# Four transformer blocks on one Trainium2 core: the reads of q and k in pieces of 16 rows and the rest

## The chip, the cores and the metric

The kernel runs on one core of one Trainium2 chip. The metric is the device time of one execution in microseconds; times here are the median of three runs. A core has TensorE (matrix products), VectorE, ScalarE and GpSimd for the rest of the arithmetic, SyncE (SP), which in this kernel does nothing but issue transfers and wait, and sixteen DMA engines that move the bytes.

## The reference

The input is 32 sequences of 128 tokens with 144 channels, and one condition vector for each sequence. Four blocks follow one another. Each one computes six modulation vectors from the condition, then attention with 16 heads of 9 dimensions, then an MLP with 576 hidden channels:

```python
q, k, v = qkv[0], qkv[1], qkv[2]          # from modulate(norm(x)) @ w_qkv + b_qkv
attn = softmax(einsum('bhqd,bhkd->bhqk', q, k) * hd ** -0.5)
o = einsum('bhqk,bhkd->bhqd', attn, v) ...
x = x + g_msa * (o @ w_proj + b_proj)
x = x + g_mlp * mlp(modulate(norm(x)))
```

Layer 0 has a mixture of four experts, two for each token, in place of the MLP. Layer 2 normalises with the root of the mean square, also q and k of each head. In layer 3 attention goes over the 16 heads of one token, `einsum('nthd,ntkd->nthk', q, k)`, so the kernel computes it for 8 tokens at once with a mask, and rearranges q, k and v through memory in pieces of 32 values.

## The kernel before, in words

The 32 sequences stay in the on-chip memory (`X`) through all four layers. They are worked in groups of four sequences, 8 groups a layer, so 32 groups over the kernel, numbered n = 0 to 31. The order of the work is written out by hand for each engine.

For attention, TensorE makes q and k with 96 rows of (dimension, head) by 512 tokens. Each value is cut into three bfloat16 parts (`parts`), whose products together give the accuracy of float32. The scores of one head then need the parts of q and k of that head on neighbouring partitions: a combination of six pairs of parts times 9 dimensions, 54 rows. That rearrangement goes through memory. `write_parts(l, n)` (line 398) writes `parts` to `qk_scr` (to `tok_scr` in layer 3), SP waits until the writes have landed (line 433), and `read_parts(l, n)` (line 421) reads them back into `qk`, for each half s (heads 0 to 7 on partitions 0 to 53, heads 8 to 15 on partitions 64 to 117) and each side (q, k). `RUNS` says which parts follow one another on the 54 rows: for q it is a run of 2 parts, one of 3 and one of 1, for k of 3, 1 and 2, with 9 rows a part. A run is one transfer, of 18, 27 or 9 rows. In the first three layers a row is 8 KB in one piece; in layer 3 it is eight pieces of 1 KB. One group has 3 x 2 x 2 = 12 read transfers and 216 rows.

`qk` has three places (n % 3), and a read is issued two groups ahead of its use. TensorE waits for both halves before the first scores of a group (`scores_for_max`, the matmuls of line 648), and `write_parts` two groups later waits for them before it overwrites the memory. Both waits are for the count that `fetched(n)` gives: each transfer adds 16 to the semaphore of its place and half.

SP's queue in a group of attention is: write the parts, wait for them, read them, in layer 3 wait for the v of the group and read it back turned (`turn_values`, line 451), load the gates (line 394), and in some groups weights (lines 344 to 356). In layer 3 ScalarE issues the writes of v (`v_scr`), and SP's wait for them is line 450.

Of the kernel before, what the change touches and what calls it, by code (L numbers as in the profile page):

```python
# [16 lines left out]
H, D = 16, 9  # L17
# [89 lines left out]
def build(nc, io):  # L107
    ctx = ExitStack()
    with ctx:
# [3 lines left out]
        def sem(name):  # L113
            return ctx.enter_context(nc.semaphore(name))
# [130 lines left out]
        q_r = [[sem(f"q_r{r}{s}") for s in range(2)] for r in range(3)]  # L245
# [38 lines left out]
        def written(n):  # L284
            return 64 * (n + 1) if n < 24 else 64 * 24 + 192 * (n + 1 - 24)

        def fetched(n):
            return 96 * (n // 3 + 1)

        def normal(k):  # L290

# [16 lines left out]
        def _(sp):  # L308
# [89 lines left out]
            def write_parts(l, n):  # L398
                p = n % 2
                if n >= 2:  # L400
                    for s in range(2):
                        sp.wait_ge(q_r[(n - 2) % 3][s], fetched(n - 2))
                for m in range(3):
                    sp.wait_ge(a_p1, CR + 3 * n + m + 1)
                    sp.wait_ge(g_p2, CR + 3 * n + m + 1)
                    sp.wait_ge(g_p3, CR + 3 * n + m + 1)
                    for side in range(2):
                        a = max(0, QK_DIMS * m - D * side)
                        b = min(D, QK_DIMS * (m + 1) - D * side)
                        if a >= b:  # L410
                            continue
                        r0 = H * (a + D * side) - QK_ROWS * m
                        src = parts[r0:r0 + H * (b - a), m]
                        if l < 3:
                            sp.dma_start(qk_scr[p, side, :, a:b].rearrange("a d h t -> (d h) a t"), src).then_inc(q_w, 16)
                            continue
                        for part in range(3):
                            sp.dma_start(tok_scr[p, side, :, :, part, a:b].rearrange("c b d h w -> (d h) (c b) w"),  # L418
                                         src[:, part].rearrange("r (a w) -> r a w", w=32)).then_inc(q_w, 16)

            def read_parts(l, n):
                p, r = n % 2, n % 3
                if 1 <= n < 3:
                    sp.wait_ge(d_mod, CR + L)
                    sp.wait_ge(s_mod, CR + L)
                if n >= 3:
                    sp.wait_ge(s_st, CR + 8 * (n - 2))
                    sp.wait_ge(s_sm, CR + 8 * (n - 2))
                if n == 26:
                    sp.wait_ge(s_v, CR + 2 * 26)  # L430
                if n in (8, 10):
                    sp.wait_ge(d_hg, CR + NT * (1 if n == 8 else 8))
                sp.wait_ge(q_w, written(n))
                for s in range(2):
                    for side, runs in enumerate(RUNS):
                        row = 64 * s
                        for first, many in runs:
                            if l < 3:
                                src = qk_scr[p, side, first:first + many, :, 8 * s:8 * s + 8].rearrange("a d h t -> (a d) (h t)")
                                dst = qk[row:row + many * D, side, r].rearrange("r h t -> r (h t)")  # L440
                            else:
                                src = tok_scr[p, side, 2 * s:2 * s + 2, :, first:first + many] \
                                    .rearrange("c b a d h w -> (a d) (c b) (h w)")
                                dst = qk[row:row + many * D, side, r]
                            sp.dma_start(dst, src).then_inc(q_r[r][s], 16)  # L445
                            row += many * D

            def turn_values(n):
# [17 lines left out]
            def attention(l):  # L466
                n0, m0 = 8 * l, 16 * l
                if l == 0:
                    write_parts(0, 0)
                    read_parts(0, 0)  # L470
                    for i in range(L):
                        save_gates(i)
                    write_parts(0, 1)
                    read_parts(0, 1)
                    sp.wait_ge(q_gs[0], 16)
                    load_gates(0)
                    sp.dma_start(X[:, 4 * G:B, :], xv[:, 4 * G:B, :]).then_inc(q_x4, 16)
                    for i in range(NEAR, NST + NEAR):
                        load_chunk(i)
                    for i in range(1, L):  # L480
                        sp.wait_ge(q_gs[i], 16)
                if l == 2:
                    write_parts(l, n0 + 1)
                    read_parts(l, n0 + 1)
# [57 lines left out]
        def _(pe):  # L542
# [97 lines left out]
            def scores_for_max(l, U):  # L640
                n = U // UNITS
                pe.wait_ge(d_sm, CR + U)
                if U % UNITS == 0:
                    for s in range(2):
                        pe.wait_ge(q_r[n % 3][s], fetched(n))
                for i in range(4):
                    for s in range(2):
                        mm = pe.matmul(bank[s][:, T * i:T * i + T], operand(l, 0, n, U, s, i),  # L648
                                       operand(l, 1, n, U, s, i), start=True, stop=True)
                mm.then_inc(s_sm, 1)  # L650
# [1462 lines left out]
```

## Time and profile before

| | |
|---|---|
| median of 3 runs | 1574.65 us (1568.06 to 1575.15) |
| profiled execution | 1567.82 us, span 1566.0 us |
| mean granted TensorE clock | 0.956 of full speed |
| busy share: VectorE, ScalarE, GpSimd | 66%, 50%, 35% |
| moved by DMA | 134.92 MB, 86 GB/s over the span |
| packets under 512 B | 142461 of 209128 |

The profile is one execution. Its span runs from the first to the last instruction, and every row below gives times from the start of the span. The DMA share is the mean busy share of the sixteen DMA engines; it can be a little over 1 because the packets of one engine overlap.

### The profile page before, as it was taken

The page shows a single profiled execution, that of the slowest core. Times are in us where ns is not written, and L with a number is a line of the kernel's source. Part 1 is how long each engine was busy: PE and PEld are TensorE (multiplying, and loading weights), DVE is VectorE, ACT ScalarE, POOL GpSimd, SP SyncE. Part 2 cuts the span into 40 slices and gives each one's busy share as a digit, 9 for nine tenths or more (in the row PEclk, how much of TensorE's full clock was granted, in tenths as well). Part 3 has the DMA queues.
Part 4 walks back from the last instruction along what each step waited for, and adds up shares of the span by engine and source line. Part 5 has one row for each costly group of instructions (what it writes and reads, how often), then busy time and mean ns, then how long its engine had stood idle before and what let it go on. Part 6 is the DMA issues. An engine that isn't in the chain of part 4 may idle for free. (4 is left out here: it accounts for less than half of the span.)

```text
span 1566.0 us, 41002 instructions
## 1 busy us (share of the span) xinstructions
PE 1427.5 (91%) x15976; PEld 1076.4 (69%) x15976; DVE 1038.6 (66%) x2592; ACT 781.2 (50%) x1287; POOL 543.8 (35%) x739
## 2 busy tenths in 40 slices
PE   6799988999999998998999778877999799998998
PEld 2477776777777776766776557666777577767776
DVE  4688874766676677878547679887446466665342
ACT  2377753333323336766645356665544265655443
POOL 3355532211131213544324323443335244342322
PEclk9799999999999999999999888998999799999999
DMA  4665631111022123554001333443116667774021
GB/s 131 159 152 145 160 79 52 50 43 43 35 68 71 38 67 81 147 131 131 17 31 35 107 88 93 108 118 98 33 36 88 110 102 111 137 134 93 17 61 46
DMA packets 209128, 134.92 MB, mean 86 GB/s; under 512 B 142461, under 2 KB 191320, under 8 KB 202730
## 3 DMA queue, kind: packets, MB, share of 16 engines
q1 hardware_dynamic: 188978, 129.74, 34.8%
q10 hardware_dynamic: 19960, 2.57, 1.2%
q8 instruction: 129, 2.11, 0.6%
q14 instruction: 61, 0.50, 0.1%
HBM read 98.24 MB, written 33.24 MB: 84 GB/s over the span
## 5 line engine op out<-in xcount | busy, mean ns | idle before, releaser
L1530 DVE TENSOR_REDUCE negm<-banks 128x8 bf16<-128x1024 f32 x256 | 311.2, 1216 | 88.7 <-PE banks L648 86.4
L1221 ACT ACTIVATE prob<-banks 128x1024 f32<-128x1024 f32 x256 | 262.3, 1025 | 212.7 <-PE banks L670 211.8
L1348 ACT ACTIVATE hid<-banks 128x512 f32<-128x512 f32 x144 | 85.9, 597 | 230.4 <-PE banks L949 230.4
L1947 POOL TENSOR_TENSOR X<-X,gx 128x288 f32<-128x288 f32 x128 | 104.9, 832 | 266.5 <-DVE gx L1560 264.7
L666 PE MATMUL banks<-qk 54*128 54x128 bf16 (+1 forms) x2048 | 172.3, 239 | 6.8 <-ACT prob L1221 5.0
L965 PEld LDWEIGHTS banks<-wfc,hid 128*128 128x128 f32 x1152 | 157.1, 190 | 30.0 <-issue 19.9
L670 PE MATMUL banks<-mT,identb 64*128 64x128 bf16 x2048 | 168.8, 228 | 0.0
L965 PE MATMUL banks<-wfc,hid 128*128 128x144 f32 x1152 | 161.5, 286 | 0.0
L648 PE MATMUL banks<-qk 54*128 54x128 bf16 (+1 forms) x2048 | 124.9, 245 | 39.7 <-DVE negm L1530 21.9
L948 PE MATMUL banks<-hT,wfc 128*128 128x512 f32 x288 | 149.0, 599 | 1.8 <-DMA wfc<-in_L_cond_w 1.3
L682 PE MATMUL banks<-prob,V 128*32 128x128 f32 x4096 | 148.4, 289 | 0.0
L1718 DVE TENSOR_TENSOR hid<-hid,qk 128x512 f32<-128x512 f32 x128 | 88.9, 695 | 88.8 <-ACT hid L1348 80.3
L1468 DVE TENSOR_SCALAR hmod<-banks,modr 64x128 f32<-64x128 f32 x256 | 86.8, 395 | 76.8 <-PE banks L581 76.4
L1932 POOL CAST parts<-res 96x512 bf16<-96x512 f32 x96 | 58.6, 611 | 212.3 <-DVE res L1481 211.4
L1373 ACT ACTIVATE hid<-banks 128x512 f32<-128x512 f32 (+1 forms) x120 | 71.1, 596 | 122.0 <-PE banks L939 121.6
L985 PE MATMUL banks<-wfc,hid 128*128 128x144 f32 (+1 forms) x960 | 130.5, 293 | 0.2 <-DVE gx L1560 0.2
L985 PEld LDWEIGHTS banks<-wfc,hid 128*128 128x128 f32 (+1 forms) x960 | 126.1, 196 | 3.8 <-issue 2.7
L648 PEld LDWEIGHTS banks<-qk 54*128 54x128 bf16 (+1 forms) x2048 | 71.1, 103 | 83.3 <-issue 38.6
L938 PE MATMUL banks<-hT,wfc 128*128 128x512 f32 x240 | 123.5, 595 | 0.0
L682 PEld LDWEIGHTS banks<-prob,V 128*32 128x32 f32 x4096 | 110.5, 115 | 17.9 <-issue 7.4
L666 PEld LDWEIGHTS banks<-qk 54*128 54x128 bf16 (+1 forms) x2048 | 110.4, 103 | 10.7 <-ACT prob L1221 7.3
L1934 POOL TENSOR_TENSOR parts<-res,parts 96x512 bf16<-96x512 f32 x96 | 112.9, 1176 | 7.9
(165 smaller groups left out, 2789.9 us busy)
## 6 DMA issues: line engine op xcount, KB each, us to landing
qk<-qk_scr SPq DMA_DIRECT2D x96, 216.0 KB
gbuf<-gate_scr SPq DMA_DIRECT2D x64, 288.0 KB, 4.2
qk_scr<-parts SPq DMA_DIRECT2D x48, 288.0 KB, 2.9
qk<-qk_scr SPq DMA_DIRECT2D x96, 144.0 KB
qk<-cw_scr SPq DMA_DIRECT2D x8, 1024.0 KB, 4.6
qk_scr<-parts SPq DMA_DIRECT2D x48, 144.0 KB, 2.4
qk<-qk_scr SPq DMA_DIRECT2D x96, 72.0 KB
qk<-tok_scr SPq DMA_DIRECT2D x32, 216.0 KB
```

The costliest lines, as they stand in the source:

```text
L648: mm = pe.matmul(bank[s][:, T * i:T * i + T], operand(l, 0, n, U, s, i), operand(l, 1, n, U, s, i), start=True, stop=True)
L666: pe.matmul(bank[2 + s][:, at], operand(l, 1, n, U, s, i), operand(l, 0, n, U, s, i), start=True, stop=False)
L670: mm = pe.matmul(bank[2 + s][:, at], one_hot(half, 64 * s + 4 * (u % 2) + i, [64, T]), mT[half, u // 2, :], start=False, stop=True)
L682: mm = pe.matmul(bank[4][32 * i:32 * i + 32, T * (2 * s + u % 2):T * (2 * s + u % 2 + 1)], V[:, n % 3, u // 2, VS * h:VS * h + 32], prob[: ...
L938: pe.matmul(bank[2 + i % 2][:], wfc1_t[:, at:at + 128], hT[:, h, :], start=True, stop=False)
L948: pe.matmul(bank[2 + i % 2][:], w, hT[:, h, :], start=True, stop=False)
L965: mm = pe.matmul(bank[4 + b // 2][:, C * (b % 2):C * (b % 2) + C], hid[:, i % KT, T * b:T * b + T], wfc2[:, e - (t == KT - 1), t, :], star ...
L985: mm = pe.matmul(bank[4 + q][:, C * (b % 2):C * (b % 2) + C], hid[0:rows, t, T * b:T * b + T], wfc2[0:rows, k, t, :], start=(t == 0), stop ...
L1221: act.activation(prob[:, 2 * (U % 3):2 * (U % 3) + 2, :], pairs[1][:], ACT.Exp, scale=scale).then_inc(a_exp, 1)
L1530: dve.tensor_reduce(negm[:, u // 2, :, 4 * (u % 2):4 * (u % 2) + 4], pairs[0][:].rearrange("q s (h k) -> q s h k", k=T), AX.X, ALU.max, ne ...
L1934: pool.tensor_tensor(parts[:, m, 2, :], res[:, i % 2, :], parts[:, m, 1, :], ALU.subtract).then_inc(g_p3, 1)
L1947: pool.tensor_tensor(x, x, gx[:, q, :, :], ALU.add).then_inc(g_x, 1)
```

## The change

A run of more than one part is no longer read by one transfer. It is cut after its 16th row: 27 rows become 16 and 11, and 18 become 16 and 2. A run of 9 rows stays whole. A group then has 5 transfers instead of 3 for each half and side, 20 instead of 12, and the count waited for rises accordingly. The rows, their places and their bytes are the same.

```diff
         def fetched(n):
-            return 96 * (n // 3 + 1)
+            return 160 * (n // 3 + 1)
...
                                 dst = qk[row:row + many * D, side, r]
-                            sp.dma_start(dst, src).then_inc(q_r[r][s], 16)
+                            for rows in (slice(0, 16), slice(16, many * D)) if many > 1 else (slice(0, D),):
+                                sp.dma_start(dst[rows], src[rows]).then_inc(q_r[r][s], 16)
                             row += many * D
```

On SP, the read of the first group begins as follows before the change. `18x4096` is a transfer of 18 rows of 4096 values; the rows shown are half 0 and the first of half 1.

```order
L445 DMA qk<-qk_scr 18x4096
L445 DMA qk<-qk_scr 27x4096
L445 DMA qk<-qk_scr 9x4096
L445 DMA qk<-qk_scr 27x4096
L445 DMA qk<-qk_scr 9x4096
L445 DMA qk<-qk_scr 18x4096 x2
```

The same place in the changed kernel, half 0 alone:

```order
L446 DMA qk<-qk_scr 16x4096
L446 DMA qk<-qk_scr 2x4096
L446 DMA qk<-qk_scr 16x4096
L446 DMA qk<-qk_scr 11x4096
L446 DMA qk<-qk_scr 9x4096
L446 DMA qk<-qk_scr 16x4096
L446 DMA qk<-qk_scr 11x4096
L446 DMA qk<-qk_scr 9x4096
L446 DMA qk<-qk_scr 16x4096
L446 DMA qk<-qk_scr 2x4096
```

Six transfers of a half have become ten, and the order of the runs is the same.

The second place is SP's queue behind a read of layer 3, group 29, before the change. `hid<-v_scr` is the read of the turned v, `gbuf` holds the gates, and `wfc` is a weight.

```order
L445 DMA qk<-tok_scr 27x8x512
L445 DMA qk<-tok_scr 9x8x512
L445 DMA qk<-tok_scr 18x8x512
L451 DMA hid<-v_scr 36x4x512
L394 DMA gbuf<-gate_scr 128x576
L349 DMA wfc<-in_L_cond_fc_w 128x4x144
```

And in the changed kernel:

```order
L446 DMA qk<-tok_scr 16x8x512
L446 DMA qk<-tok_scr 11x8x512
L446 DMA qk<-tok_scr 9x8x512
L446 DMA qk<-tok_scr 16x8x512
L446 DMA qk<-tok_scr 2x8x512
L452 DMA hid<-v_scr 36x4x512
L394 DMA gbuf<-gate_scr 128x576
L349 DMA wfc<-in_L_cond_fc_w 128x4x144
```

What is queued behind the read stays in its order and stands eight transfers later. The other engines' instructions are the same in kind and order.

## Rows read from the trace of the kernel before

**Rows 1.** The page: busy us of each engine, share of the span, instructions.

```profile
PE 1427.5 (91%) x15976; PEld 1076.4 (69%) x15976; DVE 1038.6 (66%) x2592; ACT 781.2 (50%) x1287; POOL 543.8 (35%) x739
```

**Rows 2.** Waits of PE: line, waited for: us in total, times, longest us.

```profile
PE banks L655 <- DVE On L1548: 42.7, 39, 4.3
PE banks L648 <- DVE negm L1530: 21.9, 23, 4.8
PE banks L648 <- DMA qk<-qk_scr: 8.6, 4, 3.2
PE banks L648 <- DMA qk<-tok_scr: 7.1, 3, 3.5
```

**Rows 3.** Timeline of PE: start us, us, instruction, [idle before <- releaser].

```profile
99.24 0.40 PE L648 MATMUL banks<-qk 54*128 54x128 bf16 x8 [1.48 <-DMA qk<-qk_scr]
213.50 0.49 PE L648 MATMUL banks<-qk 54*128 54x128 bf16 x8 [2.50 <-DMA qk<-qk_scr]
743.83 0.40 PE L648 MATMUL banks<-qk 54*128 54x128 bf16 x8 [1.41 <-DMA qk<-qk_scr]
1092.39 0.61 PE L648 MATMUL banks<-qk 54*128 54x128 bf16 x8 [3.19 <-DMA qk<-qk_scr]
1374.82 0.64 PE L648 MATMUL banks<-qk 62*128 62x128 bf16 x8 [2.32 <-DMA qk<-tok_scr]
1404.31 0.64 PE L648 MATMUL banks<-qk 62*128 62x128 bf16 x8 [1.27 <-DMA qk<-tok_scr]
1434.09 0.65 PE L648 MATMUL banks<-qk 62*128 62x128 bf16 x8 [3.48 <-DMA qk<-tok_scr]
```

**Rows 4.** Windows: stretch, engines' busy us, then PEclk, DMA share, GB/s.

```profile
741.20:743.80 2.60, 0.23 (x1) 0.10 (x1) 1.68 (x5) 0.38 (x1) 0.00 (x0) 1.00 0.13 34
212.00:213.50 1.50, 0.00 (x1) 0.03 (x1) 0.00 (x0) 0.00 (x0) 0.00 (x0) 1.00 0.37 107
865.00:877.50 12.50, 11.23 (x60) 8.04 (x59) 9.12 (x29) 5.62 (x14) 1.85 (x4) 1.00 0.55 142
250.00:251.00 1.00, 1.00 (x3) 0.48 (x3) 0.00 (x0) 0.43 (x1) 0.00 (x0) 1.00 0.96 401
10.00:12.00 2.00, 2.00 (x4) 0.33 (x4) 0.00 (x0) 0.00 (x0) 0.00 (x0) 1.00 1.07 353
198.00:203.00 5.00, 4.90 (x107) 4.42 (x109) 4.90 (x14) 3.44 (x6) 4.03 (x6) 1.00 0.57 159
203.00:208.00 5.00, 4.60 (x97) 3.46 (x93) 4.50 (x10) 3.35 (x5) 1.71 (x3) 1.00 0.89 173
110.00:114.00 4.00, 3.67 (x89) 2.99 (x84) 3.40 (x6) 2.88 (x4) 3.23 (x6) 1.00 0.95 172
```

**Rows 5.** Timeline of SP's queue: issues of a read, and what follows one.

```profile
864.17 4.33 SPq L445 DMA_DIRECT2D qk<-qk_scr  x12
1360.11 5.61 SPq L445 DMA_DIRECT2D qk<-tok_scr  x12
1370.38 0.29 SPq L451 DMA_DIRECT2D hid<-v_scr  x1
```

**Rows 6.** Line 445: issues, ns min/median/max of one, first and last start.

```profile
L445 SPq DMA_DIRECT2D qk<-qk_scr x288: 270/316/1250, 35.1 to 1082.0; - x144
```

**Rows 7.** Waits of SP's queue.

```profile
SPq L394 <- DVE gx L1560: 358.8, 27, 30.2
SPq L406 <- POOL parts L1934: 147.4, 64, 19.0
SPq L450 <- DMA v_scr<-wfc: 43.7, 6, 9.5
```

**Rows 8.** Chain that ended last, around group 31: start us, us, what.

```profile
1392.88 9.72 DMA v_scr<-wfc
...
1418.61 0.27 SPq L445
...
1424.45 9.50 DMA qk<-tok_scr
```

## The prediction

> **What bounds the kernel now.** I first read the busy times of the page: TensorE is busy 91% of the span and the next engine 66% [rows 1], so what the span can lose quickly is idle time of TensorE. I then asked what TensorE waits for [rows 2]. The longest waits are for VectorE (42.7 us on `On`, 21.9 us on `negm`), and the change touches neither. Waits for the reads of q and k come to 8.6 us in the first three layers (4 times) and 7.1 us in the last (3 times), 15.7 us or 1.0% of the span. The seven waits one by one are in [rows 3]; the reader is to look at the number in brackets, the idle time in front of the first scores of a group. They are 1.48, 2.50, 1.41, 3.19, 2.32, 1.27 and 3.48 us. The other 25 of the 32 groups have their q and k in time. So whatever happens to the reads, a gain is bounded by about 15.7 us, while a loss is bounded by nothing so small, since all 32 groups could come to wait.
>
> One of the seven doesn't count. In front of 743.83 the DMA engines are already nearly empty from 741.20 on (share 0.13) [rows 4], 2.6 us before TensorE starts. That read had landed, and the wait is put down to it only because no later releaser is on record. The others are real: in front of 213.50, for one, 212.00 to 213.50 still has a share of 0.37 and 107 GB/s [rows 4]. That leaves six, with 14.2 us.
>
> Next I asked how long a read takes. The cleanest one is issued from 864.17 on [rows 5], and from 865.00 to 877.50 it is nearly alone: 12.5 us at 142 GB/s, which is its 216 rows of 8 KB (1.77 MB) [rows 4]. I take 12.6 us. The waited reads are no shorter: the last one lasts from its first issue at 1418.61 to its landing at 1433.95, 15.3 us [rows 8].
>
> **The share of the DMA engines tells how many of them work.** In the clean read it is 0.55 [rows 4]; 0.55 x 16 is 8.8, so nine engines carry the read. Nine is also the largest number up to sixteen that divides 27, 18 and 9. Where tensors of 128 rows move, the share is 0.96 (the gates spread over all rows, 401 GB/s) or 1.07 (the first weights, 353 GB/s) [rows 4]: all sixteen. Read so, a transfer of 16 rows takes sixteen engines, one of 11 rows eleven, one of 2 rows two.
>
> The Trainium skill states this rule, in "DMA: Bandwidth & Descriptors", section "Why a DMA increments its semaphore by 16 and not by 1": the number of engines is the largest up to 16 that divides the slowest dimension of both sides. By that rule the trace agrees, with nine busy engines.
>
> **The change part by part.** (a) Load per engine. For each half and side there are now 2 + 3 + 1 = 6 rows on each of nine engines, 24 a group. Afterwards the first two engines carry 1 + 1 + 1 + 1 + 1 = 5 rows for each half and side, 20 a group, the next seven 16, and the last five 8. If the rate of one engine is the limit, a read shrinks by 4/24 of 12.6 us, 2.1 us.
>
> Is that rate the limit? 142 GB/s over 8.8 engines is 16 GB/s for each. In the spreading of the gates it is 401 / (0.96 x 16) = 26 GB/s for each [rows 4]. So an engine in these reads runs at 0.62 of what it can do: it is held up by something the nine have in common. A stretch where the other seven have work too says the same: from 203 to 208, while gates and weights move beside the read, the share rises to 0.89 but the rate only from 159 to 173 GB/s, and from 110 to 114 it is 0.95 with 172 GB/s [rows 4]. Half as many engines again gave 9% more bytes. What all these reads have in common is that they write 54 neighbouring partitions of one half of the memory at a time; the weights, with 353 GB/s, write 128.
>
> The Trainium skill has a rule for this that speaks against the change, in "SBUF — State Buffer", section "Door 1: The DMA port swizzle": the DMA side has 16 ports, four neighbouring partitions and the four that lie 32 further share one, and partitions 0 to 63 reach only eight. By its figures (about 436 GB/s over 16 ports, 27 GB/s for one) the busiest port takes 8 rows for each half and side, 32 rows of 8 KB a group, in about 9.6 us as an estimate, however many engines send. The sum would be 0 to -3 us a read by it, against -2.1 by load; no run here has shown it yet.
>
> So what a read's length becomes is not shown by the trace before. The bound below is -2.1 us (load alone). The bound above is one where a transfer costs the same whatever its size: 12.6 / 12 = 1.05 us each, eight more of them, +8.4 us. I take -0.5 us, near the stretches of 159 to 173 GB/s, which let a fuller set of engines have a little more.
>
> (b) Issue. SP issues 12 transfers in 4.33 us [rows 5], 0.36 us each (median 316 ns and a gap) [rows 6]. Eight more are 2.9 us; in the last layer, at 5.61 us for 12 [rows 5], up to 3.7 us. The issue of 20 ends at 20 x 0.36 = 7.2 us, in the last layer at 9.4 us; the first packets move 0.9 us after the first issue (864.17 to 865, rows 4 and 5), and the read itself needs 12 us, so the issue lies beside the packets and doesn't set the landing. Cost: 0.
>
> (c) What is queued behind it on SP: the load of the gates, weights, in the last layer the read of the turned v (L451), then the next writes. All of these start 2.9 to 3.7 us later where SP was not waiting. But it mostly waits: 358.8 us for `gx` and 147.4 us for `parts` in one of its waits [rows 7]. The gates queue behind the read's packets on the engines anyway. In the last layer SP is the chain: v to memory (9.72 us), then the writes of q and k and their landing, the read (9.50 us after its last issue) [rows 8]. There it waits for v in front of L451, 43.7 us over 6 groups [rows 7], 7.3 us on average; the issue of one read ends at 1365.72 and L451 starts at 1370.38 [rows 5], 4.66 us later. 3.7 us fits under that. Cost: 0; if that cover were gone, up to 3.7 us for each of the three waited groups of this layer, 11 us.
>
> (d) No instruction of TensorE, VectorE, ScalarE or GpSimd changes, and the counts waited for are raised with the number of transfers (5 x 2 sides x 16 = 160 for 3 x 2 x 16 = 96), so no wait is added.
>
> **The sum.** Six waited reads x -0.5 us = -3.0 us, and 0 for the rest. The profiled execution took 1567.82 us (span 1566.0 us), which makes 1564.8 us. The median of the three runs before is 1574.65 us, 6.8 us above the profiled one, and I put the forecast on that scale: 1574.65 - 3.0, rounded, 1571.6 us.
>
> **The rivals.** *The engines' load is the limit after all.* Each read takes 2.1 us less, and each wait shrinks by the smaller of itself and 2.1: 1.48 + 2.1 + 2.1 + 2.1 + 1.27 + 2.1 = 11.2 us. Something is late next in part of them (VectorE's `negm` is waited for 23 times, rows 2), so about 10 us: 1564.6 us. For it: the share of 0.55 shows seven idle engines. Against it: 16 GB/s for an engine that does 26 elsewhere.
>
> *The rows collide.* A transfer of 16 rows sends sixteen engines at 16 neighbouring rows at once, where nine engines now start three rows apart over 27. If what is shared is a path into neighbouring partitions, as the low rate suggests, the crowding costs more than the four rows save, and eight more transfers add starts and completions. A read that takes 2.0 us more (a quarter of the way to +8.4) makes all seven waits of rows 3 longer by 2.0 us, 14 us: 1588.6 us. It decides from the point where a read takes longer than 12.6 us plus what little is left before TensorE asks, which is nothing at six places. For it: 0.89 of the engines busy gave 173 GB/s, 12 GB/s each. Against it: bytes in total did not fall there. By the section on the ports named above, such a transfer would use four ports, which is the worst case of that rule.
>
> *The change doesn't spread.* Engines stay as many as now, for instance because the division follows something else than the rows; then only (b) and (c) remain, and the time is that of before, 1574.65 us.
>
> **How the numbers follow.** Forecast (reads 0 to 1 us shorter) 0.5, load as the limit 0.2, collision 0.2, no spreading 0.1. A difference under 0.5%, 7.9 us, can't be told from none here. Faster by more: 0.7 of the load case and a tenth of the forecast's, 0.19. Slower by more: 0.8 of the collision case, 0.16. Within: 0.65. The forecast alone has 1566 to 1578 us, given that the three runs before lie 7.1 us apart. The range of 8 in 10 takes in the load case down to 1560 us and the collision case up to 1585 us.
>
> **What would show it.** The share of the DMA engines in a clean read (the one near 865 us) should rise from 0.55, first near 1 and then falling, while its rate stays between 140 and 175 GB/s: then the shared limit is right. If the read ends within 10.5 us at 170 GB/s or more, the load case is right; over 14 us, the collision. SP should show 20 issues in about 7 us. The waits for `qk` should stay near 15.7 us with the forecast, fall to about 5 with the first rival and rise towards 30 with the second. In the last layer L451 should still be released by v: if SP comes to it late instead, (c) was wrong. The forecast as a whole is wrong if the reads' length stays and the time still moves by over 8 us.

## The result, and the profile after

| | before | after |
|---|---|---|
| median of 4 runs, same chip | 1571.36 us (1567.2 to 1575.15) | 1618.28 us (1614.0 to 1621.12) |
| profiled execution | 1567.82 us, span 1566.0 us | 1617.82 us, span 1616.0 us |
| mean granted TensorE clock | 0.956 | 0.944 |

The ratio is 1.0309 [1.0279, 1.034]: the change makes the kernel 3.1% slower. The forecast was 1571.6 us with a range of 1560 to 1585 us; it was wrong, and the time lies far above even the collision rival's 1588.6 us.

The busy times of the page after, to compare with [rows 1]:

```profile
PE 1443.0 (89%) x15976; PEld 1085.7 (67%) x15976; DVE 1039.2 (64%) x2592; ACT 780.4 (48%) x1287; POOL 542.5 (34%) x739
```

What TensorE waits for (line, waited for: us in total, times, longest us), to compare with [rows 2]; the scores are now line 649:

```profile
PE banks L656 <- DVE On L1549: 43.6, 40, 4.3
PE banks L649 <- DMA qk<-qk_scr: 31.8, 14, 5.9
PE banks L649 <- DVE negm L1531: 22.1, 24, 4.6
PE banks L649 <- DMA qk<-tok_scr: 15.6, 4, 7.0
```

The waits for VectorE have hardly moved. The waits for reads of q and k have gone from 15.7 us in 7 places to 47.4 us in 18. That is 31.7 of the 50.0 us by which the profiled executions differ. TensorE's busy time rose by another 15.5 us (1427.5 to 1443.0) with the same 15976 instructions, at a mean clock of 0.944 in place of 0.956: 1427.5 x 0.956 / 0.944 is 1445.6, so the lower clock is large enough to account for it. Together that is 47.2 of 50.0 us. The clock granted behind a long new wait is low. At the first scores of group 2, which wait 1.48 us before and 5.03 us after, it is 1.00 before and 0.50 after:

```profile
99.20:101.20 2.00, 1.96 (x57) 1.69 (x58) 1.23 (x1) 1.03 (x2) 1.55 (x2) 1.00 0.56 172
103.50:105.50 2.00, 1.93 (x36) 1.73 (x40) 1.22 (x1) 0.43 (x1) 0.00 (x0) 0.50 0.64 220
```

So a new wait can cost more than its own length. Not all of the 15.5 us need be of that kind: by the tables of stages below 11.6 us of them lie in the four stretches that hold the reads. The mean clock also differs between executions of one kernel, from 0.944 to 0.949 for the change and, in a kernel with no longer waits than before (e5 below), from 0.946 to 0.957.

The first scores of some groups on TensorE's timeline (start us, us, instruction, [idle before <- releaser]), to compare with [rows 3]:

```profile
103.57 0.61 PE L649 MATMUL banks<-qk 54*128 54x128 bf16 x8 [5.03 <-DMA qk<-qk_scr]
223.46 0.61 PE L649 MATMUL banks<-qk 54*128 54x128 bf16 x8 [3.42 <-DMA qk<-qk_scr]
644.84 0.40 PE L649 MATMUL banks<-qk 54*128 54x128 bf16 x8 [2.34 <-DMA qk<-qk_scr]
1129.17 0.61 PE L649 MATMUL banks<-qk 54*128 54x128 bf16 x8 [5.94 <-DMA qk<-qk_scr]
1484.04 0.64 PE L649 MATMUL banks<-qk 62*128 62x128 bf16 x8 [6.99 <-DMA qk<-tok_scr]
```

Four of the five are in the place of one of before: 1.48 us became 5.03, 2.50 became 3.42, 3.19 became 5.94, 3.48 became 6.99. The one at 644.84 is new, as are ten others. There the same eight matmuls take 0.40 us behind a wait of 2.34 us, and 0.61 us at 103.57 behind one of 5.03 us, where they took 0.40 before [rows 3].

Where in the program the time went, by stage. The columns are those of [rows 4]. A packet is counted in the stretch in which it starts, with all its time and bytes, so share and rate of a stretch of one or two microseconds are rough. Each stretch runs from the first scores of a layer's first group to those of its last. Before, layers 0 to 3:

```profile
53.60:213.50 159.90, 141.57 (x2495) 106.25 (x2495) 133.64 (x273) 104.00 (x151) 78.40 (x99) 0.95 0.62 152
...
893.60:1092.40 198.80, 154.99 (x2578) 125.19 (x2579) 168.88 (x392) 117.24 (x195) 71.43 (x112) 0.88 0.40 104
```

And after:

```profile
54.10:223.50 169.40, 142.88 (x2496) 107.32 (x2498) 133.78 (x273) 103.99 (x151) 78.88 (x100) 0.94 0.78 144
591.30:764.80 173.50, 153.82 (x2563) 116.20 (x2562) 134.51 (x268) 106.14 (x155) 74.83 (x96) 0.97 0.58 111
916.40:1129.20 212.80, 159.30 (x2578) 128.20 (x2580) 169.07 (x392) 116.98 (x195) 71.24 (x112) 0.85 0.52 98
1265.70:1484.00 218.30, 193.76 (x2585) 144.09 (x2584) 131.06 (x266) 110.93 (x163) 75.38 (x99) 0.91 0.78 114
```

Attention of layer 0 took 159.90 us and takes 169.40, that of layer 2 took 198.80 and takes 212.80; layers 1 and 3 (166.30 and 204.90 us before) take 7.2 and 13.4 us more. That is 44 of the 50 us in the four stretches that hold the reads. The DMA share rose in each, from 0.62 to 0.78 in layer 0, while the rate fell from 152 to 144 GB/s: the engines are busy longer with fewer bytes a second.

The read of group 16, before in [rows 4] from 865.00 on:

```profile
889.70:905.90 16.20, 14.92 (x92) 11.84 (x92) 11.71 (x41) 7.03 (x16) 3.05 (x9) 1.00 0.78 128
```

It takes 16.2 us in place of 12.5, with a share of 0.78 in place of 0.55. But its row is no longer of the read alone. SP issues the load of the gates 11.7 us after the read's first issue, and 113 of its 128 packets start before the read ends; in the kernel before its packets came when the read was over. The read's own 1.77 MB in 16.2 us are 109 GB/s, not 128. The next read, of group 17, has nothing beside it in either kernel. Before, as a whole, its first ten microseconds and the rest:

```profile
895.80:908.10 12.30, 4.99 (x70) 3.24 (x72) 8.85 (x14) 1.02 (x1) 0.00 (x0) 0.52 0.54 140
895.80:905.80 10.00, 3.20 (x42) 1.98 (x44) 7.13 (x12) 0.00 (x0) 0.00 (x0) 0.53 0.57 147
905.80:908.10 2.30, 1.79 (x33) 1.26 (x30) 1.72 (x3) 1.02 (x1) 0.00 (x0) 0.50 0.43 107
```

And after:

```profile
919.20:935.20 16.00, 9.34 (x119) 6.76 (x123) 12.55 (x23) 3.32 (x5) 0.00 (x0) 0.50 0.71 110
919.20:929.20 10.00, 3.84 (x50) 2.36 (x50) 7.20 (x11) 0.00 (x0) 0.00 (x0) 0.50 0.89 139
929.20:935.20 6.00, 5.50 (x69) 4.40 (x73) 5.35 (x14) 3.32 (x5) 0.00 (x0) 0.50 0.41 63
```

It takes 16.0 us in place of 12.3, so the gates aren't the reason. The rows to look at are the two of ten microseconds. With 0.89 of the sixteen engines busy they move 139 GB/s, where nine engines (0.57) moved 147: many more engines at work, and no more bytes. What is left after ten microseconds then goes slowly, 63 GB/s at a share of 0.41.

From the packet records, each read from its first to its last packet (216 rows, or 1728 pieces of 1 KB in layer 3): a read of the first three layers lasts 13.46 us on average before and 16.25 us after, one of layer 3 13.2 and 15.6 us. The mean packet of 8 KB stays on its engine for 526 ns before and 799 ns after. These two numbers nearly give the length of a read: the busiest engine had 24 rows and now has 20 by the prediction's count, and as an estimate 24 x 526 ns is 12.6 us and 20 x 799 ns is 16.0 us. The load fell by a sixth, and each packet takes half as long again.

SP's queue, to compare with [rows 5], and its line in the form of [rows 6]:

```profile
888.78 7.27 SPq L446 DMA_DIRECT2D qk<-qk_scr  x20
1402.59 8.39 SPq L446 DMA_DIRECT2D qk<-tok_scr  x20
1412.24 0.29 SPq L452 DMA_DIRECT2D hid<-v_scr  x1
L446 SPq DMA_DIRECT2D qk<-qk_scr x480: 220/308/1685, 35.6 to 1119.1; - x160
```

SP's waits, to compare with [rows 7]:

```profile
SPq L394 <- DVE gx L1561: 362.1, 27, 30.3
SPq L451 <- DMA v_scr<-wfc: 31.3, 6, 8.5
```

And the chain that ended last at group 31, to compare with [rows 8], where the last step was 9.50 us:

```profile
1473.29 10.61 DMA qk<-tok_scr
```

### The profile page after: what moved, and what is told of

Same layout as the page of the kernel before. It is cut to its first block and busy times, and to the rows that moved or that the text cites. A ratio compares the mean times of both kernels' runs of the same rounds, so it can differ in the third digit from the quotient of the medians.

```text
span 1616.0 us, 41258 instructions
## 1 busy us (share of the span) xinstructions
PE 1443.0 (89%) x15976; PEld 1085.7 (67%) x15976; DVE 1039.2 (64%) x2592; ACT 780.4 (48%) x1287; POOL 542.5 (34%) x739
## 5 line engine op out<-in xcount | busy, mean ns | idle before, releaser
L649 PE MATMUL banks<-qk 54*128 54x128 bf16 (+1 forms) x2048 | 126.2, 247 | 71.5 <-DMA qk<-qk_scr 31.8
L667 PE MATMUL banks<-qk 54*128 54x128 bf16 (+1 forms) x2048 | 174.9, 240 | 7.8 <-ACT prob L1222 5.0
L683 PE MATMUL banks<-prob,V 128*32 128x128 f32 x4096 | 153.8, 295 | 0.4 <-issue 0.4
L683 PEld LDWEIGHTS banks<-prob,V 128*32 128x32 f32 x4096 | 113.9, 117 | 19.7 <-issue 8.9
L667 PEld LDWEIGHTS banks<-qk 54*128 54x128 bf16 (+1 forms) x2048 | 112.5, 104 | 11.2 <-ACT prob L1222 7.3
L1165 ACT ACTIVATE hT<-banks,modm 128x128 f32<-128x128 f32 x256 | 99.5, 453 | 34.9 <-PE banks L575 34.9
```

Source lines behind the costliest of these rows:

```text
L667: pe.matmul(bank[2 + s][:, at], operand(l, 1, n, U, s, i), operand(l, 0, n, U, s, i), start=True, stop=False)
L683: mm = pe.matmul(bank[4][32 * i:32 * i + 32, T * (2 * s + u % 2):T * (2 * s + u % 2 + 1)], V[:, n % 3, u // 2, VS * h:VS * h + 32], prob[: ...
L1165: act.activation(hT[:, slot_of(k), T * b:T * b + T], bank[o][:, T * b:T * b + T], ACT.Identity, scale=modm[:, l, 2 * w + 1, at:at + 1], bi ...
```

## The experiments

Each was timed against the kernel before on its own chip, and each diff is against the kernel before. Read lengths and packet times are means worked out from the packet records as above; the waits are TensorE's in front of the scores (in e5 and e8 the trace puts them down to the tiny transfers, which count on the same semaphore). A table first, to have the sizes side by side:

| kernel | ratio to before | read, layers 0 to 2 | 8 KB packet | waits |
|---|---|---|---|---|
| before | 1 | 13.5 us | 526 ns | 15.7 us |
| the change | 1.0309 [1.0279, 1.034] | 16.25 | 799 | 47.4 |
| e1_nine_pieces | 1.025 [1.0206, 1.0295] | 16.0 | 629 | 31.7 |
| e2_spread_sixteen | 1.0492 [1.0446, 1.0537] | 16.2 | 443 | 64.9 |
| e3_spread_nine | 1.0016 [0.9995, 1.0037] | 13.4 | 432 | 15.4 |
| e4_one_source_row | one run, 1638.52 us | 16.7 | 830 | 54.8 |
| e5_eight_tiny | 1.0033 [1.0003, 1.0062] | 13.7 | 526 | 15.6 |
| e8_slow_issue | one run, 1638.12 us | 17.4 | 734 | 64.3 |
| e6_halves_in_turn | 0.991 [0.9887, 0.9933] | 11.9 | 468 | 4.2 |
| e7_sixteen_in_turn | 1.0081 [1.0055, 1.0107] | 15.4 | 754 | 26.0 |
| e9_crossed | 0.994 [0.9918, 0.9962] | 12.3 | 481 | 3.0 |
| e10_only_27 | 1.0077 [1.0046, 1.0108] | 14.25 | 652 | 18.4 |
| e11_only_18 | 1.0277 [1.024, 1.0314] | 15.9 | 672 | 38.3 |
| e12_ten_eight | 1.0086 [1.0059, 1.0113] | 14.4 | 565 | 22.9 |
| e13_even_cuts | 1.0278 [1.0237, 1.0319] | 16.2 | 728 | 38.9 |
| e14_turn_15_12 | 0.9963 [0.9936, 0.999] | 13.3 | 618 | 7.9 |

**Twenty transfers, nine engines.** Is it the sixteen engines? The runs are cut at their last 9 rows, so every transfer has 9 or 18 rows.

```diff
+for rows in (slice(0, many * D - D), slice(many * D - D, many * D)) if many > 1 else (slice(0, D),):
+    sp.dma_start(dst[rows], src[rows]).then_inc(q_r[r][s], 16)
```

> Twenty transfers a group as in the changed kernel, but cut after a multiple of nine rows (27 = 18 + 9, 18 = 9 + 9), so that nine engines carry each one. Theory N (each further transfer costs by itself, in issue and completion): as slow as the changed kernel, about 1.03 of before, a clean read of about 16 us. Theory D (sixteen engines at sixteen neighbouring partitions at once crowd the way into them): about the time of before, ratio 1.00 to 1.01, a clean read of 12.5 to 13.5 us at a DMA share of 0.55.

Measured: 1603.86 us, and a read of group 16 of 17.0 us:

```profile
885.80:902.80 17.00, 15.73 (x96) 12.54 (x95) 12.25 (x42) 7.75 (x18) 3.11 (x5) 1.00 0.62 119
```

Theory D in this form, which ties the crowd to sixteen engines, is refuted, and theory N has its numbers; it falls with e5 below. Nine engines with equal loads are nearly as slow as sixteen with unequal ones. So neither the number of engines nor the uneven load is needed for the loss. In these pieces of 9 rows nine engines write nine neighbouring partitions at a time. That in a run of 27 rows they stand three apart is the prediction's reading; the packet records name neither engine nor partition.

**The destinations spread.** The 54 rows of a half are laid on every third partition, in pieces of up to 16 rows, or of up to 18 rows (nine engines). q and k are laid out alike, so the scores are the same sums.

```diff
+at = 0
+while at < many * D:
+    c, i = divmod(row - 64 * s, 18)
+    m = min(many * D - at, 18 - i)
+    m = 16 if m == 18 else m          # e2 only
+    p0 = 64 * s + c + 3 * i
+    dst = qk[p0:p0 + 3 * m - 2:3, side, r]
```

> Pieces of 16, 2 and 9 rows, twenty-four transfers a group, with the 54 rows laid in every third partition (row 18c + i of a half on partition c + 3i, for q and k alike, so the scores are the same), so that sixteen engines write to partitions three apart over 46. Theory D: the read falls well under the changed kernel's 16.1 us, to 10 to 13 us, and the ratio to before is at or below 1.01. Theory N: slower still than the changed kernel, 1.03 to 1.05, reads of 17 us or more. Theory S (the source: sixteen neighbouring rows of memory at once are slow): as the changed kernel, 1.03.

> Same spread partitions, nine engines, pieces of 18 and 9 rows, sixteen transfers a group. Theory D: the transfers of 9 rows no longer meet on three groups of four partitions, a clean read falls from 12.5 us to 11 to 12 us, ratio 0.992 to 1.000. Theory N: four more transfers than before, a quarter to a half of the changed kernel's loss, 1.01 to 1.015. If the neighbours of a partition play no part at all: 12.5 us and 1.00.

Measured: 1642.6 and 1570.05 us. The first doesn't test what it was made for, and SP's issues show why (the second line is the same of e2 as [rows 5]):

```profile
L451 SPq DMA_DIRECT2D qk<-qk_scr x576: 496/622/1527, 35.3 to 1133.3; - x192
899.05 15.64 SPq L451 DMA_DIRECT2D qk<-qk_scr  x24
```

A transfer that steps three partitions at its destination takes SP 622 ns to issue instead of 316, so 24 of them take 15.6 us, and the 16.2 us of the read are the issue. For e3 the issue of 16 takes 11.90 us, and its read of group 16 takes 12.9 us, not the 11 to 12 us of theory D. What both do show is the packet: with destinations three apart, 443 ns for 8 KB with sixteen rows to a transfer and 432 ns with nine engines, against 799 and 526. But packets that come slowly meet less company, which needs a control.

**The control: the change's pieces, issued slowly.** Behind each of the twenty transfers a tiny one (2 rows of 8 bytes) is issued.

```diff
+sp.dma_start(dst[rows], src[rows]).then_inc(q_r[r][s], 16)
+bit = src[0:2, 0:4] if l < 3 else src[0:2, 0, 0:4]
+sp.dma_start(tiny[:, c:c + 4], bit).then_inc(q_r[r][s], 16)
```

> The changed kernel with a tiny transfer (2 rows of 8 bytes) behind each of its twenty, so that the pieces of 16 rows on neighbouring partitions are issued at about 0.66 us each, the pace of the kernel with spread partitions and sixteen engines. There a packet of 8 KB took 443 ns on average, against 799 ns in the changed kernel. Theory D: packets stay at 650 to 800 ns here. If the slow issue alone had relieved them: 430 to 500 ns. The time is bound by 40 issues, 13 us and more a read, in either case, 1615 to 1660 us.

Measured, in one run: 1638.12 us, packets of 734 ns, though the issue of a read is stretched to 13.0 us. e2, at 15.9 us for 24 transfers, has nearly the same pace (0.66 us each against 0.65) and 443 ns. So the neighbourhood of the destinations lengthens the packets, and the pace is a small part. That the read itself got longer (17.4 us) speaks against a cure by slower issue.

**One source row for all.** The change's pieces, but each transfer reads its first row again and again. The values of q and k are therefore not the reference's.

```diff
+one = src[rows.start:rows.start + 1].to_broadcast([rows.stop - rows.start] + list(src.shape[1:]))
+sp.dma_start(dst[rows], one).then_inc(q_r[r][s], 16)
```

> The changed kernel with every read transfer taking all its rows from its first source row: same transfers, same destination partitions, only one row of memory a transfer is read, so the values of q and k are not the reference's. Theory S: the reads fall to 8 to 11 us and the time to 1565 us or less. Theories D and N: the reads stay at about 16 us and the time at 1600 to 1620 us.

Measured, in one run: 1638.52 us, packets of 830 ns, read 16.7 us. The time lies 20 us above the change, beyond what any theory had. It is no better than the change, so where the rows lie in memory isn't the cause, if a single repeated row is not itself a difficulty. It isn't: when the gates are spread (one 8 KB row to 128 partitions by sixteen engines, the 401 GB/s of [rows 4]), a packet takes 309 ns in the median and 344 ns on average. A single source row with neighbouring destinations takes 830 ns. That leaves the destination.

**Eight more transfers, tiny.** The twelve reads as before, with eight transfers of 9 rows of 16 bytes among them.

```diff
+if many > 1:
+    bit = src[0:D, 0:8] if l < 3 else src[0:D, 0, 0:8]
+    sp.dma_start(tiny[:, j:j + 8], bit).then_inc(q_r[r][s], 16)
```

> The kernel before, with its twelve transfers untouched, and eight tiny ones beside them (9 rows of 16 bytes each, after every transfer of 18 or 27 rows, to a spare place), so twenty transfers a group are issued and counted as in the changed kernel. Theory N (a transfer costs by its issue, start and completion, whatever it carries): most of the changed kernel's loss, 1.02 to 1.03, reads of 15 to 16 us. Theory D (crowding: which partitions the engines write at the same time): no more than the spread of the runs, 1.00 to 1.005, reads of 13 to 14 us with packets of about 530 ns.

Measured: ratio 1.0033 [1.0003, 1.0062], packets 526 ns, clean read 12.4 us:

```profile
872.40:884.80 12.40, 11.13 (x59) 7.94 (x59) 9.12 (x29) 5.51 (x14) 2.25 (x5) 1.00 0.54 142
```

The row is that of before. The count of transfers, with its issue and its waits, is worth at most 0.6%; the 1.05 us for a transfer that made the upper bound is ruled out.

**The halves in turn.** If neighbouring destinations are what is crowded, transfers to the two halves of the partitions should go beside each other better than two to the same half. Only the order of the twelve transfers changes: half 0 and half 1 alternate.

```diff
-for s in range(2):
-    for side, runs in enumerate(RUNS):
+for side, runs in enumerate(RUNS):
+    for first, many in runs:
+        for s in range(2):
```

> The kernel before with the same twelve transfers in another order: a run of half 0 (partitions 0 to 53), then the same run of half 1 (64 to 117), instead of all of half 0 first. Theory D, if the crowding is on paths that the two halves don't share: reads fall from 13.4 to 10 to 12 us and the ratio is 0.985 to 0.998. Theory N, or a crowding that the halves share: 13.4 us and 1.00.

Measured: 1556.88 us, ratio 0.991 [0.9887, 0.9933]. It beats both kernels. Two reads of it, groups 16 and 17:

```profile
862.90:874.20 11.30, 10.03 (x52) 6.94 (x51) 8.74 (x29) 5.55 (x14) 1.67 (x4) 1.00 0.52 155
892.20:902.70 10.50, 4.31 (x58) 2.69 (x58) 7.29 (x11) 0.57 (x1) 0.00 (x0) 0.50 0.53 165
```

and what is left of the waits:

```profile
PE banks L649 <- DMA qk<-qk_scr: 2.4, 1, 2.4
PE banks L649 <- DMA qk<-tok_scr: 1.8, 1, 1.8
```

Still nine engines (0.52 x 16 is 8.3), the same bytes, and 155 to 165 GB/s. The waits fall by 11.5 us and the profiled time by 12.0 us (1567.82 to 1555.85); the medians are 14.0 us apart (1570.86 and 1556.88). It is more than the 10 us of the prediction's most favourable rival, and without a further engine. The Trainium skill's rule in "SBUF — State Buffer", "Door 1: The DMA port swizzle", agrees in direction: halves have ports of their own. The prediction's estimate by its figures, 9.6 us for one half after the other, doesn't give the change's loss, since the same rows go to the same ports before and after, and the reads take 13.5 and 16.25 us.

**The change with the halves in turn, and with the sides crossed.** e7 is the change's twenty pieces in the order of e6. e9 is the twelve whole transfers, alternating, with q going to one half while k goes to the other.

```diff
+# e7
+for rows in (slice(0, 16), slice(16, many * D)) if many > 1 else (slice(0, D),):
+    for s in range(2):
+# e9
+for turn in range(2):
+    for j in range(3):
+        for s in range(2):
+            side = (turn + s) % 2
```

> The changed kernel with its twenty transfers in another order: a piece of half 0, then the same piece of half 1. Theory D with separate paths of the halves: reads fall from 16.1 us to 12 to 14 us, ratio 1.00 to 1.015. Theory N: 16 us and 1.03.

> Twelve transfers, half 0 and half 1 in turn, and in addition the sides crossed: while half 0 reads a run of q, half 1 reads the run of k at the same place (18 beside 27, 27 beside 9, 9 beside 18), so that two transfers that follow one another differ in their rows too. If only the alternation of the halves counts: as that kernel, reads of about 11.9 us and 0.991. If the two transfers of 9 rows following one another were still a crowd (9 engines on 3 groups of four partitions): reads of 10.5 to 11.5 us and 0.986 to 0.991.

Measured: e7 1.0081, e9 0.994. The order alone takes back 2.3 of the change's 3.1%, but its packets remain at 754 ns and its reads at 15.4 us (13.3 us in layer 3), where theory D had 12 to 14 us. e9's interval [0.9918, 0.9962] overlaps e6's: crossing the sides adds nothing.

**Which cut?** Only the 27s are cut (16 and 11), or only the 18s (16 and 2), 16 transfers in either case.

```diff
+for rows in (slice(0, 16), slice(16, many * D)) if many == 3 else (slice(0, many * D),):   # e10
+for rows in (slice(0, 16), slice(16, many * D)) if many == 2 else (slice(0, many * D),):   # e11
```

> Only the runs of 27 rows are cut (16 and 11), those of 18 stay whole, sixteen transfers a group. Theory D (a piece with one neighbouring row for each engine is the crowd): the cut puts 27 of the 54 rows into such pieces, beside the 9 that already were, so about 27/43 of the changed kernel's lengthening, reads near 15 us, ratio 1.013 to 1.022.

> Only the runs of 18 rows are cut (16 and 2), those of 27 stay whole, sixteen transfers a group. Theory D: 18 of 54 rows move into such pieces, a smaller lengthening than with the 27, reads near 14.3 us, ratio 1.005 to 1.015. The two together should about make the changed kernel's 1.031.

Measured: 1.0077 and 1.0277, reads of group 16 of 14.7 and 16.0 us. Theory D had the larger loss at the 27s, and it is the other way round: the cut of the 18s alone makes nine tenths of the whole loss. Its waits are:

```profile
PE banks L649 <- DMA qk<-qk_scr: 24.1, 11, 6.0
PE banks L649 <- DMA qk<-tok_scr: 14.2, 3, 6.6
```

Only a part of e10's loss is waits for reads: they rise by 2.7 us, the profiled time by 11.2 us, and 5.8 us more is idle time of TensorE for which the profile names no releaser ("issue"). What that is stays open.

The packet records have a candidate for e11. If row j of a transfer goes to engine j (the records don't name the engine), pieces of 2 rows give their work to engines 0 and 1. In e11 these carry 24 rows a read, the next seven 20, and seven engines 4. In the last three microseconds of the read of group 16, 5.3, 2.5 and 1.2 engines are busy and 8, 5 and 4 rows are finished, where before has 9.1, 8.6 and 5.8 busy and finishes 18, 18 and 14.

**The same cuts without the pieces of 2.** e12 cuts 18 into 10 and 8 alone; e13 does that and cuts 27 into 15 and 12, twenty transfers again.

```diff
+for rows in (slice(0, 10), slice(10, 18)) if many == 2 else (slice(0, many * D),):   # e12
+cut = {1: D, 2: 10, 3: 15}[many]                                                     # e13
+for rows in (slice(0, cut), slice(cut, many * D)) if many > 1 else (slice(0, D),):
```

> Only the runs of 18 rows are cut, but into 10 and 8 instead of 16 and 2; 27 stay whole, sixteen transfers a group as with the cut into 16 and 2, which took 1.028 of before. Theory D (one neighbouring row for each engine is a crowd): 18 of 54 rows are in such pieces in both kernels, so about the same here, reads of 15 to 16 us, 1.02 to 1.03. Theory T (the pieces of 2 rows leave a tail: engines 0 and 1 carry 24 rows, the other seven 20, and at the end only two engines work): no tail here, since engines 0 to 7 carry 24 each, so reads near 13.5 us and 1.000 to 1.010.

> Both runs cut without small remainders: 27 = 15 + 12 and 18 = 10 + 8, twenty transfers, all with one neighbouring row for each engine; engines 0 to 7 carry 20 rows, engine 8 has 16. Theory D: as the changed kernel, reads near 16 us, 1.025 to 1.035. Theory T: reads near 14 us, 1.005 to 1.015, as when only the 27 are cut.

Measured: 1.0086 and 1.0278, with reads of group 16 of

```profile
868.90:882.80 13.90, 12.63 (x71) 9.44 (x71) 10.06 (x32) 6.99 (x17) 2.89 (x5) 1.00 0.55 132
```

and

```profile
889.80:906.50 16.70, 15.42 (x96) 12.29 (x95) 11.71 (x41) 7.03 (x16) 3.55 (x9) 1.00 0.70 124
```

With 10 and 8 in place of 16 and 2 the loss falls from 2.8 to 0.9% (e11 against e12), and the thin tail is gone from the records of e12. That is what theory T had, but it doesn't show the tail to be the cause: the cut also sends ten engines at once instead of sixteen, and the packets are shorter, 565 against 672 ns. The busiest engines have 24 rows in both, and 24 x 565 ns is 13.6 us, 24 x 672 ns 16.1 us as an estimate, near the reads of 14.4 and 15.9 us. And e13 is as slow as the change within 0.3%, without a piece of 2 rows: its last microseconds have 8.0, 8.0, 3.7 and 0.6 engines busy with 8, 8, 9 and 2 rows finished, so that a packet of its pieces of 8 rows takes a full microsecond. A tail of two rows isn't needed for a loss; whether it makes one by itself is not shown. The parts don't add up either: 0.8 and 0.9% make 2.8% (e10, e12, e13, though e13 cuts the 27s at another row than e10), 0.8 and 2.8% make 3.1% (e10, e11, the change).

**The best order with a mild cut.** The 27s cut into 15 and 12, halves in turn.

```diff
+for rows in (slice(0, 15), slice(15, 27)) if many == 3 else (slice(0, many * D),):
+    for s in range(2):
```

> Halves in turn (0.991 of before, reads of 11.9 us on nine engines) and the 27 rows cut into 15 and 12, so that nine engines carry 20 instead of 24 rows and the others help. If the load of nine engines has become the limit once the halves alternate: reads of 10 to 11 us, 0.985 to 0.991. If neighbouring single rows crowd here too: reads of 12.5 to 14 us, 0.995 to 1.01.

Measured: 0.9963 [0.9936, 0.999], packets 618 ns, reads of 13.3 us, as by crowding. Worse than e6 without any cut, whose interval lies wholly below. No cut that was tried beats the whole runs in the same order.

## Why the prediction was wrong

**What bounds the kernel, and what the waits allow.** Right, but for the count of places in the sum. TensorE and its waits set the time, and 31.7 of the 50.0 us are those waits. The sentence that a loss is bounded by nothing so small was the one to weigh: 11 groups that had not waited now do. Counting from the packet records, 6 groups of before had their last row within 1 us of TensorE's use, and 19 after. The slack could have been read before the change: about 1 us passes between the last packet and the first scores even in a group that waits, and 22 of the 32 groups had less than 3.7 us, so that a read longer by 2.8 us reaches them. The sum had six. That one of the seven waits was not real is borne out: the last packet of the read in front of 743.83 ended at 741.23. After the change this group's last row is within 1 us too, and it waits 2.63 us.

**(a) The read.** This is the step that failed. The prediction took -0.5 us a read; measured are +2.8 us (13.46 to 16.25), and 3.7 us in the reads of groups 16 and 17. Its first half was right: the engines are held up by something they have in common, since the share rose to 0.71 in the read of group 17 and the rate didn't rise with it, and e4 and e5 leave the destination for it. The second half was wrong: it took the common limit as a fixed rate that a fuller set of engines keeps or betters, from stretches in which seven other engines worked on gates and weights, that is, on other partitions. At 203 to 208 "half as many engines again gave 9% more bytes" [rows 4] doesn't speak of sixteen engines that all write neighbouring partitions. With those the rate of the first ten microseconds was 139 in place of 147 GB/s, and over the whole read 110 in place of 140, as the packets took 799 in place of 526 ns.

Two slips in its working change nothing. The list of loads leaves out two engines, which have 12 rows a group. And the 32 rows for "the busiest port" add up both halves, which by the Trainium skill's section cited there have different ports: a port takes 16 rows a group, and 9.6 us holds only for one half after the other.

**(b) Issue.** Right: 20 issues in 7.27 us (7.2 forecast), in the last layer 8.39 us (9.4 forecast), and e5, with twenty issues but the reads uncut, is 0.3% slower. It would not have been for a stepping destination (e2).

**(c) The queue behind on SP.** Right in its cost. In the read at 1402.59 the issue ends at 1410.98 and line 452 is issued at 1412.24, 1.3 us later. SP still waits for v 6 times, 31.3 us in all (43.7 before), so it comes late in no group where it was early. That is 12.4 us less, no more than the 16.7 us that six reads with 2.8 us more of issue each could take from it. That the gates queue behind the read's packets was not so in the read of group 16, where they ran beside its last four microseconds; the read of group 17 was as much longer without them.

**(d) No other change.** Right for the instructions (15976 on TensorE). Not named there: TensorE's mean clock fell from 0.956 to 0.944, and 15.5 us of busy time came with it, most of it in the stretches with the longer waits. The sum had no such term, and every rival's price lacked it as well.

**The rivals.** Load as the limit: refuted, the read got longer although the busiest engine has 20 rows for 24 by the prediction's count. No spreading: refuted by the share, 0.71 of a read that is alone. The collision had the right mechanism and too small a size: +2.0 us against +2.8, seven waits against 18, "towards 30" against 47.4 us, and no clock. Of its two parts, the crowding is supported by five comparisons: e1 (nine engines on neighbouring rows), e4 against the gates' spreading, e2 against e8, and e6 and e7, where the same pieces in another order gain 0.9 and 2.3%. The other, "eight more transfers add starts and completions", is small by e5. By the prediction's own signs, a read over 14 us and waits towards 30 us or more, the collision is what came.

**Still open.** How much of the loss is crowding, and how much is engines that run out of work early: no run changes the one without the other. Why the effects of two cuts don't add, in the reads themselves too: +0.75 and +0.9 us (e10, e12) make +2.7 (e13). And what the crowded part is: the runs show it only as neighbouring partitions of one half.

## What to carry to other kernels

Before a transfer is cut to occupy more DMA engines, look at where its rows land: if the engines already run below their best elsewhere, more of them on the same neighbouring partitions move no more bytes, and the order of the transfers (halves in turn) is the cheaper thing to change. Before a step is priced only at the places where it is waited for today, count how many others have less slack than the step may lose, and add what the clock loses behind each new long wait. Where a cut can't be avoided, its place matters: 18 rows as 10 and 8 cost 0.9%, as 16 and 2 2.8%.

## What the runs showed of the hardware

- An 8 KB packet took 799 ns on average in transfers of up to sixteen neighbouring partitions, 526 ns in the whole runs, and 344 ns (median 309) spread over 128 partitions from one source row. With 0.89 of sixteen engines busy on neighbouring partitions 139 GB/s moved, with nine engines on the whole runs 147.
- A destination that steps three partitions doubled SP's median issue time, from 316 to 622 (e2) and 684 ns (e3).
- Transfers to the two halves of the partitions in turn moved 155 to 165 GB/s through nine engines; one half after the other 140 to 142.
